# Routed experts worked out for their own tokens in pages of 128 rows, on one Trainium2 core

## What is computed

```python
scores = jax.nn.sigmoid(x @ gate_w)                  # 32 experts
topk_w, topk_i = jax.lax.top_k(scores, 6)            # 6 of them for each token
topk_w = topk_w / (jnp.sum(topk_w, -1, keepdims=True) + 1e-20)
combine = jnp.sum(one_hot(topk_i, 32) * topk_w[..., None], axis=1)
g = jnp.einsum('td,edf->tef', x, wg)                 # f = 96 hidden features an expert
u = jnp.einsum('td,edf->tef', x, wu)
routed = jnp.einsum('tef,efd,te->td', silu(g) * u, wd, combine)
shared = silu(x @ sg) * (x @ su) @ sd                # 192 hidden features, all tokens
return routed + shared
```

## Time and profile before

| | |
|---|---|
| three runs | 2017.56 us median, 2014.81 to 2021.04 us |
| profiled execution, span | 2014.2 us (its own time is not given apart from the span) |
| TensorE matmul busy | 1739.2 us, 86% |
| VectorE, GpSimd, ScalarE busy | 1108.5, 873.9 and 823.4 us |
| mean granted TensorE clock | 0.973 of full speed |
| data moved | 139.26 MB |

### The profile page before, as it was taken

One profiled execution on the slowest core, in us unless ns is written; L12 is line 12 of the kernel. 1 busy time (PEld: TensorE's weight loads), 2 busy tenths in 40 slices (PEclk: granted clock), 3 DMA queues, 4 the chain that ended last, 5 costly groups with the idle time before them and its releaser, 6 DMA issues.

```text
span 2014.2 us, 41842 instructions
## 1 busy us (share of the span) xinstructions
PE 1739.2 (86%) x16112; PEld 1338.2 (66%) x16112; DVE 1108.5 (55%) x2557; ACT 823.4 (41%) x1596; POOL 873.9 (43%) x995
## 2 busy tenths in 40 slices
PE   3647898989989888999989898998889899888887
PEld 2425676767767676776767676776767677676766
DVE  5537274655637365564836556473656647364442
ACT  2442535343353534335353433435343343534332
POOL 2321443535354354435435343544534354454555
PEclk7678999999999999999999999999999999999999
DMA  5531322313132231314123231412313141221211
GB/s 135 135 102 37 88 58 56 84 49 87 37 96 57 56 80 52 87 37 101 52 65 83 52 75 38 102 52 71 77 51 76 40 102 50 78 63 52 54 60 37
DMA packets 323318, 139.26 MB, mean 69 GB/s; under 512 B 227568, under 2 KB 308528, under 8 KB 323120
## 3 DMA queue, kind: packets, MB, share of 16 engines
q1 hardware_dynamic: 304688, 86.23, 18.6%
q0 software_dynamic: 18432, 50.36, 9.0%
HBM read 102.12 MB, written 29.88 MB: 66 GB/s over the span
## 4 chain that ended last, share of the span: by engine, by line
PE 32%; issue 20%; DVE 17%; POOL 10%; ACT 8%; SPq 8%; DMA 4%; POOLq 0%; DVEq 0%; ACTq 0%
PE s3r L1394 8%; PE s2acc L1391 5%; SPq L579 4%; POOL gs L762 3%; POOL h2l L771 3%; PE s1a L1394 2%; DVE th L1269 2%; POOL cb L741 2%; SPq L552 2%; ACT p L876 2%; DMA stacks<-part_d 2%; PE s2r L1652 2%; PE s2r L1394 2%; DVE mx L1102 2%; ACT p L936 1%
## 5 line engine op out<-in xcount | busy, mean ns | idle before, releaser
L771 POOL TENSOR_TENSOR h2l<-th,h2h 128x512 f16<-128x512 f32 (+1 forms) x224 | 246.4, 1103 | 350.5 <-ACT h2h L967 339.3
L762 POOL TENSOR_TENSOR gs<-gs,cb 128x512 f32<-128x512 f32 x192 | 243.5, 1268 | 299.9 <-DVE gs L1274 295.7
L1391 PE MATMUL s2acc<-xd,h2h 128*128 128x256 f16 x1536 | 264.3, 274 | 28.8 <-POOL h2l L771 28.8
L1394 PE MATMUL s3r<-xe,xg 128*128 128x256 f16 x2304 | 283.0, 273 | 2.5 <-DVE gs L1274 2.5
L967 ACT CAST h2h<-th 128x512 f16<-128x512 f32 (+1 forms) x224 | 131.5, 587 | 373.8 <-DVE th L1269 334.5
L1394 PE MATMUL s3r<-xe,xu 128*128 128x256 f16 x2304 | 282.9, 273 | 1.1 <-DVE th L1269 1.1
L1394 PEld LDWEIGHTS s3r<-xe,xg 128*128 128x128 f16 x2304 | 223.2, 98 | 33.0 <-DVE gs L1274 6.3
L1394 PEld LDWEIGHTS s3r<-xe,xu 128*128 128x128 f16 x2304 | 223.6, 98 | 28.2 <-DVE th L1269 1.7
L1269 DVE TENSOR_TENSOR th<-s3r,gs 128x512 f32<-128x512 f32 x192 | 132.1, 688 | 196.2 <-POOL gs L762 170.1
L741 POOL DMA_DIRECT2D cb<-comb_d x384 | 227.4, 599 | 19.5 <-issue 9.9
L1274 DVE SCALAR_TENSOR_TENSOR gs<-th,s3r 128x512 f32<-128x512 f32 (+1 forms) x224 | 144.1, 643 | 160.6 <-ACT th L971 158.8
(11 more groups left out here) (280 smaller groups left out, 3139.9 us busy)
## 6 DMA issues: line engine op xcount, KB each, us to landing
cb<-comb_d POOLq DMA_DIRECT2D x128, 192.0 KB, 3.4
part_d<-part SPq DMA_DIRECT2D x32, 512.0 KB, 3.3
cb<-comb_d POOLq DMA_DIRECT2D x128, 128.0 KB, 3.0
stacks<-part_d SPq DMA_DIRECT2D x192, 64.0 KB, 2.4
va<-v_d SPq DMA_DIRECT2D x512, 8.0 KB
cb<-comb_d POOLq DMA_DIRECT2D x128, 64.0 KB, 3.1
land<-part_d SPq DMA_DIRECT2D x96, 64.0 KB, 2.7
part<-part_d SPq DMA_DIRECT2D x96, 64.0 KB, 3.0
```

Source lines behind the costliest of these rows:

```text
L762: g.tensor_tensor(gc2[:, p % 2, :], gs2[:, p % 2, :], cb2[:, 2 * (p % 6):2 * (p % 6) + 2, :].rearrange("p a s -> p (a s)"), ALU.mult).then ...
L771: g.tensor_tensor(h2l[0:m, n % 2, 0:w], th2[0:m, n % 2, 0:w], h2h[0:m, n % 2, 0:w], ALU.subtract).then_inc(sem("h2l_made"), 1)
L1391: ins = nc.tensor.matmul(bk, lhs[i][k], rhs[j][k], start=first and chain[0], stop=last and chain[1], skip_group_check=True)
L1394: ins = nc.tensor.matmul(bk, lhs[i][k], rhs[j][k], start=first, stop=last)
```

## The change

**Pages.** The routed experts are no longer worked out for all tokens. Batches form three groups (`GROUPS = (8, 5, 3)`). Each token is copied six times, once for each of its experts, into a table in DRAM (`rows_d`) that is made of pages of 128 rows; a page belongs to one expert. A group of n batches has at most 12n + 31 pages: 127, 91 and 67. Two pages are a unit: 64, 46 and 34 units, 144 in all. The tables of the first two groups are filled with zeros at the start, by 28 transfers that ScalarE issues (`zero`).

**The router's new part** (streams 7). TensorE counts with triangular matrices how many earlier tokens chose the same expert (`rank`), GpSimd works out in 23 small dependent steps on 32 or 64 columns where each expert's next page starts (`gp7`), VectorE makes the six row numbers (`slot4`) and weights (`share4`) of each token and the list of the pages' owners (`owners3`). Then GpSimd issues 12 indirect transfers a batch, of 128 rows of 1 KB each, that scatter the tokens.

**A unit.** SyncE loads its 256 rows, TensorE turns them (8 transposes), ScalarE copies the turned rows out of PSUM, TensorE makes gate and up with 24 matmuls of 128 columns, ScalarE tanh, VectorE two products, ScalarE the float16 part, GpSimd the low part, TensorE 6 matmuls of 256 columns, ScalarE copies the result out, SyncE stores it (`y_d`). Which expert's weights are used is read by TensorE's queue from the list with two `value_load`s, and enters the matmuls' addresses through a register.

**Gathering.** After the last unit of a group has been stored, GpSimd gathers for each batch the 6 x 2 pieces of 128 rows with 12 indirect transfers into three buffers (`RING4`), and VectorE multiplies each by its weight and adds it to the sum (stream 4). That sum starts as the residual with the shared expert (`base_d`), to which the attention branch (`attn_d`) is added by an accumulating transfer.

**Order.** Stream 3 is now one list for the whole kernel: feed-forward chunks of layer 0, the shared expert, and units, at most `QUOTA[b]` in step b: none in steps 0 to 8, 13, 13, 13, 13, 12, 15 in steps 9 to 14, and 15, 16, 34 in steps 15 to 17. It has three PSUM banks of its own; stream 2 has one (`mid`); the two accumulating banks are gone. Layer 1's attention is a stream of its own (8). `ORDERS` is one string for the whole kernel on each engine. Layer 1's projection is kept and stored. The combine weights' transfer, the broadcasts (line 741) and the products with them (line 762) are gone.

```diff
+GROUPS = (8, 5, 3)
+QUOTA = {9: 13, 10: 13, 11: 13, 12: 13, 13: 12, 14: 15, 15: 15, 16: 16, 17: 34}
...
+    XPAGES = [TOP * S // P * n + NX - 1 for n in GROUPS]
+    XUNITS = [(n + 1) // 2 for n in XPAGES]
...
+        for i in range(len(order3) + 2):
+            drained = i >= 2 and order3[i - 2][0::2] == ("f", NCH - 1)
+            if i < len(order3) and order3[i][0] == "u":
+                plan.append(uses("turn", order3[i][1]))
+            if drained:
+                weigh3(order3[i - 2])
+            if 1 <= i <= len(order3):
+                plan.append(uses("in", *order3[i - 1]))
+            if i >= 2 and not drained:
+                weigh3(order3[i - 2])
...
+            for t in range(T):
+                for j in range(TOP):
+                    g.indirect_dma_start(rows_d[k % 2][:, :], bass.IndirectOffsetOnAxis(ap=slot4[:, it, t, j:j + 1], axis=0),
+                                         rows2[:, t, :, :].rearrange("p g c -> p (g c)"), None).then_inc(sem(f"scattered{k}"), 16)
+                yield
...
+        def gp4(gp):
+            g = nc.gpsimd
+            for b in range(B):
+                k = OF[b]
+                gp.wait_ge(*event("base_loaded", b, 16))
+                gp.wait_ge(*event("attn_saved", b, 16))
+                g.dma_start(sum4[:, :, :], one(attn_d, b).rearrange("b (t p) e -> p (b t) e", p=P), accum_op=ALU.add).then_inc(sem("attn_added"), 16)
+                yield
+                for t in range(T):
+                    for j in range(TOP):
+                        n = (b * T + t) * TOP + j
+                        if b == FIRST[k] and t == j == 0:
+                            for i in range(2):
+                                gp.wait_ge(*event(f"y_saved{i}", None, 16 * len(range(i, UNIT0[k + 1], 2))))
+                                carry(gp, "gp_waited")
+                        if n >= RING4:
+                            gp.wait_ge(*event("mixed", None, n - RING4 + 1))
+                        g.indirect_dma_start(got4[:, n % RING4, :], None, y_d[k][:, :], bass.IndirectOffsetOnAxis(ap=slot4[:, b, t, j:j + 1], axis=0)
+                                             ).then_inc(sem(f"got{n % RING4}"), 16)
+                        yield
...
+                if use[0] == "turn":
+                    r = use[1]
+                    act.wait_ge(*full3(use))
+                    if r >= 2:
+                        act.wait_ge(*full3(("in", "u", r - 2)))
+                    s.copy(xt3[:, r % 2, :, :, :].rearrange("p i g n -> p (i g n)"), bk[:, :].bitcast(F16)).then_inc(empties3(use), 1)
+                    yield
...
+            def turned(use):
+                r, bk = use[1], bank3(use)[:, :].bitcast(F16)
+                pe.wait_ge(*event(f"rows_loaded{r % 2}", None, 16 * (r // 2 + 1)))
+                pe.wait_ge(*free3(use))
+                for i in range(2):
+                    for k in range(4):
+                        ins = nc.tensor.transpose(bk[:, 512 * i + P * k:512 * i + P * k + P], rows3[:, r % 2, i, P * k:P * k + P], ident16[:, :])
+                ins.then_inc(fills3(use), 1)
+                g, u = group3(r)
...
+                owners[r] = [pe.value_load(owners3[0:1, g % 2, 2 * u + i:2 * u + i + 1], min_val=0, max_val=NX - 1) for i in range(2)]
+
+            def unit_in(use):
+                r, bk = use[2], bank3(use)
+                pe.wait_ge(*emptied3(("turn", r)))
+                pe.wait_ge(*free3(use))
+                for i in range(2):
+                    at = owners[r][i] * FX
+                    for c, ws in enumerate((xg, xu)):
+                        ins = parts3(bk[:, 2 * P * c + P * i:2 * P * c + P * i + P], [[w[:, k, bass.ds(at, P)] for k in range(K)] for w in ws],
+                                     [[xt3[:, r % 2, i, K * x + k, :] for k in range(K)] for x in range(2)])
+                ins.then_inc(fills3(use), 1)
...
-            run("pe", None, pe1(pe, 0), None, folding(), pe0(pe, 1), order="start")
-            run("pe", pe2(pe, 0), pe1(pe, 1), None, pe3(pe, 0, first_units), pe0(pe, 2), order="first")
...
+            play("pe", (chain(pe0(pe, b) for b in range(1, B)), chain(pe1(pe, b) for b in range(B)), chain(pe2(pe, b) for b in range(B)),
+                        pe3(pe), (), (), folding(), chain(pe7(pe, b) for b in range(B)), chain(pe8(pe, b) for b in range(B))))
```

More of the change, by code:

```diff
@@ new lines, in uses, with spread @@
+        def uses(kind, *at, hold=0):
+            b = min((b for b in range(3) if held3[b] <= len(U3)), key=lambda b: held3[b])
+            held3[b] = len(U3) + hold
+            U3[(kind, *at)] = b, taken3[b]
+            taken3[b] += 1
+            if kind == "in":
+                H3[at] = len(H3)
+            return (kind, *at)
+        def spread(steps, units):
+            out, done = [], 0
+            for i, x in enumerate(steps):
+                while done * len(steps) < units * i:
+                    out.append("u")
+                    done += 1
+                out += x
+            return out + ["u"] * (units - done)
@@ new lines, in group3, with rows_of, weighed3 @@
+        def group3(r):
+            g = next(g for g in range(len(GROUPS)) if r < UNIT0[g + 1])
+            return g, r - UNIT0[g]
+        def rows_of(at):
+            return {"f": CH_M, "s": (P, FS2), "u": (FX,)}[at[0]][at[2] if at[0] != "u" else 0]
+        AT3 = {n: at for at, n in H3.items()}
+        def weighed3(n):
+            at = AT3[n]
+            if at[0] == "u":
+                return full3(("down", *at))
+            last = {"f": NCH, "s": 2}[at[0]] - 1
+            return full3(("down", *at[0:2])) if at[2] == last else event(at[0] + "_part", at[1], at[2] + 1)
@@ L476, in two, with chain @@
+        def chain(stages):
+            for x in stages:
+                yield from x
+                yield
         def two(x):
@@ L479, in one, with play @@
         def one(x, it):
-            if isinstance(it, Before):
-                return x[bass.ds(it.it - it.back, 1)]
-            return x[it:it + 1] if isinstance(it, int) else x[bass.ds(it, 1)]
+            return x[it:it + 1]
         block = ctx.enter_context(nc.Block())
-        experts = [(kind, n) for n in range(UNITS) for kind in (("gate", "up", "down") if n else ("gate", "up"))]
-        experts = [(kind, n - (kind == "down")) for kind, n in experts] + [("down", UNITS - 1), ("out", 0)]
-        experts.insert(experts.index(("up", 1)) + 1, ("weights", 0))
-        cut = experts.index(("gate", HEAD_UNITS))
-        first_units, last_units = experts[:cut], experts[cut:]
-        def run(engine, layer1, layer0, older, newer, front, order="body"):
-            streams = (layer0, layer1, older, newer, front)
-            for turn in ORDERS[engine][order]:
-                if streams[int(turn)] is not None:
-                    next(streams[int(turn)], None)
+        def play(engine, streams):
+            streams = [iter(stages) for stages in streams]
+            for turn in ORDERS[engine]:
+                next(streams[int(turn)], None)
             for stages in streams:
-                assert stages is None or next(stages, "end") == "end"
+                assert next(stages, "end") == "end"
         def sp0(sp, it):
@@ L1000, in _ @@
             piece(0)
-            run("act", None, None, None, None, front)
+            for n in range(FRONT_STAGES):
+                next(front, None)
             for i in range(NCODE):
```

1392 lines of the change are left out of this document (796 added, 596 removed), and 10 rows, old and new, of the table PER.

## The result

The changed kernel takes 2089.74 us (median of 4 runs, 2086.0 to 2096.07) against 2016.18 us for the kernel before beside it (4 runs, 2010.18 to 2021.04): a ratio of 1.0376, 95% interval 1.0343 to 1.0408. It is slower by 3.8%, where the forecast was 13% faster and the range ended at 1945 us. The profiled execution has a span of 2088.3 us.

What follows compares the result with a forecast made beforehand. TensorE's work was taken as the bound; start 235, seven periods 504, six periods with units 616, the rest 300 and the end 90 gave 1745 us, plus 3.4 for the median: 1750 us, range 1620 to 1945.

Steps and rivals of the forecast that it cites:

- near 1350: Sign for the whole changed kernel: TensorE's busy sum would be near 1350 us at full clock.
- rival (b): In the units, weight loads set the pace of short matmuls, 0.041 us more each: 189 us, so 1940 us; chance 0.05.
- 80%: TensorE's busy share in the seven periods without units to batch 9: 72 us each, between 64 and 82.
- 92%: TensorE's busy share in the six periods with units to batch 15, 102.7 us each, and in the rest after.
- +143, +102 and +112 us of the table: Profile minus forecast for seven periods to batch 9 (504), six to batch 15 (616), then to the last unit's matmul (300).
- 540 us beside 1750, which TensorE's work covers: Scatters and gathers on GpSimd: 384 indirect transfers at 1.4 us, hidden behind TensorE's work.
- The zeroing: At the start, zeroing two tables takes 125 us of all DMA engines, hidden but for about 20 us.
- Register reads: In each unit, two reads and addresses on TensorE's queue: 0.3 us taken, between 0 and 1.2.
- 0.9 would add 6 us: Sign against the forecast: a mean clock of 0.9 adds 6 us to each of seven periods without units.
- (a): TensorE starved in the units by register reads or ScalarE's round, 4 us or more a unit: 1965 us; chance 0.12.
- (c): Better than forecast: periods without units 64 us, registers free, the end 60 us: 1620 us; chance 0.17.
- (d): GpSimd becomes the bound at the gathers, slower if a transfer costs 2.5 us or more; 2124 us at 3.0; chance 0.08.

Runs made afterwards that it cites:

- d1: The changed kernel unchanged, run again on a fourth chip as the measure for the variants beside it: 2095.06 us, 1.0398 of the kernel before.
- d2: Changed kernel with thin units, 6 matmuls each and all other work kept, beside the unchanged one: 2068.92 us, 1.0258 of the kernel before.
- c4: Changed kernel without the 28 transfers that zero the paged tables: 2043.8 us, 1.0152 of the kernel before.
- d4: Changed kernel with matmuls of zeros as fillers ahead of TensorE's waits, 239 us of added work: 2158.44 us, 1.0721 of the kernel before.
- c2: Changed kernel without indirect transfers except the first three gathers: 1985.44 us, 0.9864 of the kernel before.
- y, z and e: Sets of variants of the changed kernel, each set sharing one chip: the first eight variants (y, z), 2050.26 to 2330.17 us, and two later ones (e), 2067.26 and 2062.71.

## Why the prediction was wrong

**TensorE's work was right.** Taking half of the busy time at half clock off, the changed kernel's matmuls are 1349 us at full clock, where the sign named was "near 1350". In d1 it is 57.2 us in a period without units (forecast 57.8) and 93.1 in one with (94.5). A unit's matmuls come at 55 to 58 ns (0.057), so rival (b) is out. The Trainium skill's 81 ns for short matmuls ("TensorE: Matmul & The Clock Gate", Back-to-back issue gap) doesn't agree with this trace either. By it the units would have, as an estimate, 111 us more work.

**The step that failed is the share of TensorE.** I put "80%" on periods without units and "92%" on those with, the second because the earlier trace rows shows 91%. Measured, as work at full clock over time, are 64% and 75%. Period by period (d1):

| period | work at full clock | more by the half clock | idle | sum |
|---|---|---|---|---|
| without units, forecast | 57.8 | 0 | 14.2 | 72 |
| without units, d1 | 57.2 | 9.4 | 22.4 | 89.0 |
| with units, forecast | 94.5 | 0 | 8.2 | 102.7 |
| with units, d1 | 93.1 | 7.1 | 23.3 | 123.5 |

So the difference is more idle time and the clock, and without units the clock's part is as large as the other (9.4 us of 17). In the kernel before the share was high because TensorE was the bound: its queue had routed matmuls while the other engines worked. Those matmuls were what the change removed. With a third of a unit's matmul work (d2) or all of it the periods with units last about as long, TensorE's waits for the units' low parts grow from 50 to 126 us, and the last 34 units come 4.3 and 4.6 us apart: there the round TensorE, ScalarE, VectorE, ScalarE, GpSimd, TensorE sets the pace. That the attentions' chains do the same in the periods without units is argued from the waits and not shown by a run. Forecasting a period as work divided by the old share can't show either. These are most of the +143, +102 and +112 us of the table.

**What of it has a price by experiment:**

- The indirect transfers, "540 us beside 1750, which TensorE's work covers": their size was about right (384 x 1.27 = 488 us, and the gathers' waits for buffers beside it), the cover wasn't. Without them 105 us go. The low parts behind them in GpSimd's order are 39 us, if moved. I had charged GpSimd's total and not asked what stands behind a burst of six.
- The zeroing: 47 us and not 20. The start came right (232 for 235) by luck: without the zeroing the feed-forward of batch 2 starts at 191 us (c4), 24 us before what I had for that.
- Register reads: 30 us for 144 units, 0.2 us a unit (forecast 0.3, 43 us). The term was right in size, though the upper bound of 1.2 us for the unhidden work wasn't (1.8 us a unit). The Trainium skill's floor of some 600 ns for a `tensor_load` ("DMA: Bandwidth & Descriptors", Latency and other measured facts) doesn't agree with this trace: 288 of them take 300 ns in the median, the shortest 294.
- The clock. The text said that it would be wrong if the clock fell in the periods without units; it did, to a mean of 0.86 (d1), where "0.9 would add 6 us". In the seven periods 132 us of busy time ran at half clock, 66 us more than at full, 9 a period. So this sign came true, and its price was set too low. The runs d2 and d4 show both directions: less work lowers the clock and the time hardly falls, fillers raise it and the time rises. What the same work would take without the half clock no run shows.

**The rivals.** (a) had a mechanism that d2 bears out, a unit's round through the other engines, and 1965 us. Its "4 us or more" a unit is what the last 34 units take (4.6 us). It went short because the periods without units were too long as well: c2, with almost no indirect transfer, still has 84.7 us for a forecast of 72. (c) failed with the 64 us. (d), the one on the right side, had the wrong mechanism: 1.27 us each, and GpSimd is 62% busy in the period of batch 15 and 76% in the fullest slice of the page. Its point of decision, 2.5 us, was never near. None of the rivals was a lower share of TensorE everywhere.

**Smaller slips.** The bytes that the prediction lists add up to 261 MB and not 256; the page shows 255.86 MB. "Near 60%" for the DMA engines is 46% by the queues' shares. In the last 34 units ScalarE is not as long as TensorE: it is busy for 79 of 151 us, TensorE for 119.

**What is open.** Without indirect transfers TensorE still has only 68% of the seven periods (401 of 593 us), 13 us a period over the forecast. Which link of the attentions' chain holds them (SyncE's issues are 20% of that kernel's chain) wasn't tried. Nor was the order: the change also gave each engine one new fixed order for the whole kernel, divided the PSUM banks anew and cut the descriptor space, and no run varied the first two or gave back the third whole.

## What to carry to other kernels

- A high busy share of the bounding engine is made by the work that you are about to remove. Before dividing the rest by that share, take the round that one item makes through all engines and count how many items are under way at once; or first build a version with that work thinned out, as d2: it shows what the other engines leave of the gain, at the clock that TensorE then gets.
- On an engine that works through a fixed order, ask of each new burst not what it costs but who waits for the next instruction behind it.
- Run the unchanged kernel beside every set of variants; here y, z and e lacked it. Two of the chips here added up to 118 us to the same variants, though the kernel before took the same time on all.

## What the runs showed of the hardware

- On two of the five chips used for experiments, kernels with indirect transfers show ScalarE and VectorE standing still behind finished results of TensorE: in the first of them 68 times, 3.2 us in the mean and 10.9 at most, and 152 to 222 us in sum in six of the eight, some 85% of it while GpSimd issues such transfers. The same kernels on the other chips show none: low parts on VectorE 2174 and 2056 us, thin units 2118 and 2069, fillers 2235 and 2158, constant owners 2133 and 2063. The kernel before, with no indirect transfer, took 2013 to 2015 on all five. Why the chips differ is not known; the changed kernel itself was not run on those two.
- Thinning TensorE's work by about 125 us in a stretch lowered its mean clock from 0.92 to 0.85 and shortened the stretch by 15 us.
- Twice the descriptor space doesn't shorten the 1.27 us from an indirect transfer of 128 rows to the next instruction, but the idle times of over 1 us ahead of such transfers fall from 10 (30 us) to 4 (12 us).
- A register read by TensorE's queue (`TENSOR_LOAD`) takes 300 ns in the median of 288, the check of its bounds another 151; of 256 us of such queue work some 30 reached the time.
